# Four graph layers on one core: where roots, weight scales, kept pairs, block sums and score rows stand in the engines' order

## What is computed

```python
h = jnp.maximum(_layernorm(x, axis=-1), 0.0)
x = x + relu(dinv * (adj + I) * dinv.T @ h @ W0)                      # layer 0, dinv from row sums + 1
x = x + (dis * adj * dis.T @ h) @ W1.T + b1                           # layer 1, dis from row sums
x = x + relu(A_norm @ h @ W2)                                         # layer 2, adj + I, normalized
hw = h @ W_sa; scores = s_left[:, None] + s_right[None, :]            # layer 3, from hw
e = where(adj != 0, exp(-leaky_relu(scores, 0.01)), 0)
x_a = (e / (e.sum(1) + 1e-5)) @ hw;  x_b = adj @ (h @ W_gcnb) + b_gcnb
x = x + sigmoid(attn_a * x_a + attn_b * x_b)                          # attn_a, attn_b: sigmoid gates of adj @ h and h
```

## Time and profile before

| | |
|---|---|
| Time, median of three | 1823.18 us (1820.59 to 1827.55) |
| Profiled execution | 1826.1 us |
| Its span from first to last instruction | 1824.3 us |
| PE busy | 1710.0 us, 94% of the span |
| DVE busy | 1117.9 us, 61% |
| ACT busy | 772.5 us, 42% |
| POOL busy | 608.5 us, 33% |
| DMA | 418.91 MB, mean 230 GB/s |

### The profile page before, as it was taken

How to read it: one execution, slowest core, us unless ns; L and a number is a source line. 1 busy time by engine, 2 the same in 40 slices (tenths; PEclk the granted TensorE clock), 3 DMA queues, 4 the chain that set the end, 5 groups by cost and what they waited for, 6 DMA issues and landing times.

```text
span 1824.3 us, 31720 instructions
## 1 busy us (share of the span) xinstructions
PE 1710.0 (94%) x12862; PEld 1165.6 (64%) x12862; DVE 1117.9 (61%) x1957; ACT 772.5 (42%) x1178; POOL 608.5 (33%) x567
## 2 busy tenths in 40 slices
PE   3999898898899998999999999999999899999996
PEld 1444343655678886868877897887888544444454
DVE  5776978875676665634534443454641667877765
ACT  5665545543443433412322231310110567768654
POOL 0001636353645453522302120111210445545431
PEclk9999999999999999999999999999999999999998
DMA  9984679778958787995575798767645443444423
GB/s 393 359 308 150 217 267 316 248 277 315 329 198 294 266 308 232 326 349 209 169 251 176 227 323 312 269 216 239 224 142 170 135 127 96 147 129 119 145 85 124
DMA packets 185720, 418.91 MB, mean 230 GB/s; under 512 B 18245, under 2 KB 79041, under 8 KB 181841
## 3 DMA queue, kind: packets, MB, share of 16 engines
q1 hardware_dynamic: 185572, 416.88, 66.6%
HBM read 305.64 MB, written 111.17 MB: 228 GB/s over the span
## 4 chain that ended last, share of the span: by engine, by line
PE 67%; DVE 14%; DMA 7%; ACT 5%; POOL 3%; issue 2%; SPq 1%; ACTq 0%; DVEq 0%; POOLq 0%
PE ps L1109 13%; PE ps L1154 11%; PE ps L1156 11%; PE ps L1155 11%; PE ps L1201 7%; PE ps L1203 6%; PE ps L1202 6%; DVE U L1454 4%; DMA U<-in_adjT 3%; DMA Ad<-U 2%; ACT U L1782 1%; DMA U<-in_adj 1%; POOL U L1960 1%; DMA HB<-in_wg 1%; DVE stage L1437 1%
## 5 line engine op out<-in xcount | busy, mean ns | idle before, releaser
L1154 PE MATMUL ps<-U,HB 128*128 128x256 f16 (+2 forms) x2520 | 634.4, 260 | 7.0 <-DVE U L1454 3.6
L1155 PE MATMUL ps<-U,HB 128*128 128x256 f16 (+2 forms) x2520 | 634.2, 260 | 0.0
L1156 PE MATMUL ps<-U,HB 128*128 128x256 f16 (+2 forms) x2520 | 634.1, 260 | 0.0
L1201 PE MATMUL ps<-U,HB 128*128 128x512 f16 (+3 forms) x960 | 343.9, 361 | 47.4 <-DVE U L1454 34.7
L1202 PE MATMUL ps<-U,HB 128*128 128x512 f16 (+3 forms) x960 | 342.7, 360 | 0.0
L1203 PE MATMUL ps<-U,HB 128*128 128x512 f16 (+3 forms) x960 | 342.4, 359 | 0.0
L1454 DVE SCALAR_TENSOR_TENSOR U<-U,cS 128x512 f16<-128x512 f32 (+7 forms) x255 | 253.2, 1018 | 124.3 <-ACT U L1782 123.8
L1109 PE MATMUL ps<-W,OT 128*128 128x512 f16 (+1 forms) x1320 | 303.7, 384 | 15.5 <-DVE xr L1523 9.0
L1782 ACT ACTIVATE U<-U,cS 128x512 f16<-128x512 f32 (+7 forms) x255 | 197.5, 802 | 177.8 <-POOL U L1960 57.5
L1154 PEld LDWEIGHTS ps<-U,HB 128*128 128x128 f16 x2520 | 246.2, 98 | 36.5 <-DVE U L1454 3.8
L1155 PEld LDWEIGHTS ps<-U,HB 128*128 128x128 f16 x2520 | 246.4, 98 | 26.1
(11 more groups left out here) (204 smaller groups left out, 1954.7 us busy)
## 6 DMA issues: line engine op xcount, KB each, us to landing
U<-Ad SPq DMA_DIRECT2D x85, 896.0 KB, 6.5
U<-in_adjT SPq DMA_DIRECT2D x289, 256.0 KB, 4.6
Ad<-U SPq DMA_DIRECT2D x34, 896.0 KB, 5.8
xd<-xr SPq DMA_DIRECT2D x84, 256.0 KB, 5.7
HB<-HBd SPq DMA_DIRECT2D x24, 896.0 KB, 8.7
xr<-xd SPq DMA_DIRECT2D x84, 256.0 KB, 5.3
U<-in_adj SPq DMA_DIRECT2D x14, 1354.0 KB, 8.6
U<-Ad SPq DMA_DIRECT2D x23, 707.0 KB, 5.0
```

The lines of the kernel that those rows point to most:

```text
L1154: eng.matmul(o, h[0], hi, start=J == 0 and a == 0, stop=False)
L1155: eng.matmul(o, h[0], lo, start=False, stop=False)
L1156: last = eng.matmul(o, h[1], hi, start=False, stop=to in "acg" and J == 9 and a == 1)
L1201: eng.matmul(o, h[0], hi, start=j == 0, stop=False)
```

## The change

Nothing that is computed changes. The list of stages does:

- `AHEAD` has 18 pairs, not 20 (the pairs (6, 6) and (8, 4) are made on the fly in pass 1). They follow one another every 7.8 planned us, not 8.5; inside a pair the sums stand at 7.5, not 5.2, the splits at 11 and 12, not 8 and 9, and the write of the finished pair at 20 (15 for the last two), not 12.5.
- The square root on ACT becomes a stage of its own, "root". For the first seven pairs of layer 1's tiles it stands 2.6 planned us behind the variance, and the norms 2.6 behind that. `quiet` is 12 everywhere, where it was 16 for these. "x_keep" stands at 9, not 10.
- The power-of-two scale of a weight matrix becomes a stage "w_scale"; the high half on ACT follows two to four steps later, and all later stages of a matrix move back.
- The restores of layer 1 are cut in two DMAs: slots 0 to 3 of `HB` (free as soon as column 5 has used them) from step (5, 2J + 2) on, slots 4 to 6 from (5, 7 + J) on. Before, both went as one from (5, 11 + J) on.
- `spaced` puts two projects, not three, into the half-wide columns 10 and 16 and four, not three, into columns 11 and 17, and moves those of columns 6, 12 and 18 forward (8, 11.5, 15, 18.5 for 9, 13, 17, 21).
- The score row of column 24 is made at step (23, 8), not (23, 13); scores, masks and splits of pass 4 may stand 17, 15 and 12 planned us ahead (15.6, 13, 10.4 before), and the masks no longer wait in the list for `acc` to be free (POOL still waits for it).

```diff
--- before.py
+++ after.py
@@ -117,7 +117,7 @@
 AHEAD = [(g, j) for g in range(GW, 12) for j in
-         ((0, 2, 4, 6) if g == GW else (0, 2, 4) if g < 11 else (0, 2, 4, 10))]
+         ((0, 2) if g == 8 else (0, 2, 4) if g < 11 else (0, 2, 4, 10))]
 def made_ahead(g, j):
@@ -277,13 +277,13 @@
     def ahead(u):
         nonlocal fetched, eyed, split, summed, scored, masked
-        while scored < len(scores) and near(scores[scored], u, 6, 15.6) and scored < masked + 2:
+        while scored < len(scores) and near(scores[scored], u, 6, 17) and scored < masked + 2:
             if not have(("row_out", scores[scored][1]), *free_of("sc_a")):
                 break
             put("score", *scores[scored][1:])
             scored += 1
-        while masked < scored and near(scores[masked], u, 5, 13) and masked < s.count.get("split_e", 0) + 3:
-            if not have(("fetch",) + scores[masked], *free_of("em"), *free_of("acc")):
+        while masked < scored and near(scores[masked], u, 5, 15) and masked < s.count.get("split_e", 0) + 3:
+            if not have(("fetch",) + scores[masked], *free_of("em")):
                 break
             put("mask", *scores[masked][1:])
             masked += 1
@@ -298,7 +298,7 @@
                 break
             put("eye", *eyes[eyed][1:])
             eyed += 1
-        while split < len(splits) and near(splits[split], u, LA, 10.4 if splits[split][1] >= GE else 9.6):
+        while split < len(splits) and near(splits[split], u, LA, 12 if splits[split][1] >= GE else 9.6):
             g, j = splits[split][1:]
             if not have(("fetch", "agg", g, j)) or splits[split] in eyes and not have(("eye", g, j)) or g < 2 and not have(("scale", g)) or g >= GE and not have(("mask", g, j)):
                 break
@@ -336,30 +336,41 @@
     def weights(n, g, *js):
-        kinds = ("w_fetch", "w_max", "w_top", "w_hi", "w_lo", "w_keep") if n else ("w_fetch", "w_max", "w_hi", "w_lo")
+        kinds = ("w_fetch", "w_max", "w_top", "w_scale", "w_hi", "w_lo", "w_keep")
+        if n == 0:
+            kinds = ("w_fetch", "w_max", "w_scale", "w_hi", "w_lo")
         for kind, j in zip(kinds, js):
             plan(AT["agg", g, 0] + j if g else AT["agg", 0, 15] + j, kind, n)
     def pair(u, l, J):
         nonlocal quiet
-        plan(max(later(u, 2.6), u + 1), "norms", l, 2 * J, 2)
-        u = max(later(u, 5.2), u + 2, quiet)
+        late = 2.6 if l == 1 and J < 7 else 0
+        if late:
+            plan(max(later(u, late), u + 1), "root", l, 2 * J, 2)
+        else:
+            put("root", l, 2 * J, 2)
+        plan(max(later(u, 2.6 + late), u + 1), "norms", l, 2 * J, 2)
+        u = max(later(u, 5.2 + late), u + 2, quiet)
         steps = [(0, "normed", l, 2 * J), (0.6, "normed", l, 2 * J + 1), (1.4, "h_sums", l, J), (5, "hi", l, J),
                  (6.5, "lo", l, J)]
         if J < 8 or l == 3 and J < 10:
             steps.append((12, "image", l, J))
         if l == 1:
             steps += [(5, "xbias", 2 * J), (5, "xbias", 2 * J + 1)]
-        steps += [(10, "x_keep", "post", l - 1, 2 * J), (10, "x_keep", "post", l - 1, 2 * J + 1)]
+        steps += [(9, "x_keep", "post", l - 1, 2 * J), (9, "x_keep", "post", l - 1, 2 * J + 1)]
         for us, *stage in steps:
             v = later(u, us)
             if J == 8 and stage[0] in ("hi", "lo", "image"):
                 v = max(v, AT["agg", 6 * l, {"hi": 1, "lo": 2, "image": 5}[stage[0]]])
             plan(v, *stage)
-        quiet = later(u, 8 if J >= 7 else 16 if l == 1 else 12)
+        quiet = later(u, 8 if J >= 7 else 12)
         if J < 8:
-            late = AT["agg", 6 * l, 4 * J - 20] if J > 5 else AT["agg", 6 * l - 1, max(2 * J + 2, 11 + J if l == 1 else 0)]
-            plan(max(later(u, 24), late), "restore", l, J)
+            gone = AT["agg", 6 * l - 1, 2 * J + 2] if J < 6 else AT["agg", 6 * l, 4 * J - 20]
+            if l > 1:
+                plan(max(later(u, 24), gone), "restore", l, J, 0, 7)
+            else:
+                plan(max(later(u, 24), gone), "restore", l, J, 0, 4)
+                plan(max(later(u, 24), gone, AT["agg", 5, 7 + J]), "restore", l, J, 4, 7)
         if l == 3 and J in (7, 9):
             plan(max(later(u, 14), AT["agg", GE - 1, 17 if J == 7 else 20]), "restore_h21", 1 if J == 7 else 2)
@@ -400,18 +411,21 @@
         g, c = now - 1, now % 6
-        at_us = {0: (9, 13, 17, 21), 4: (9, 14, 19), 5: (3, 10, 15)}.get(c, (12, 18.5, 25, 31.5))
+        at_us = {0: (8, 11.5, 15, 18.5), 4: (9, 18), 5: (3, 10, 16.5, 23)}.get(c, (12, 18.5, 25, 31.5))
+        n = 2
+        if now >= GE - 2:
+            n, at_us = 3, (9, 14, 19) if c == 4 else (3, 9, 20)
         todo = [(g, t) for t in tiles(g)]
         if c == 4:
-            todo.pop()
+            todo = todo[:n]
         if c == 5:
-            todo.insert(0, (g - 1, tiles(g - 1)[-1]))
+            todo = [(g - 1, t) for t in tiles(g - 1)[n:]] + todo
         for (f, t), us in zip(todo, at_us):
             p, v = CHUNKS[f][0], later(u, us)
             plan(v, "project", f, t, SUMS[now]["x"])
             if p < 3:
                 if c or t not in tiles(g)[:2]:
-                    plan(max(u + 1, later(u, us - 9)), "x_load", "post", p, t)
+                    plan(max(u + 1, later(u, us - (9 if c else 6))), "x_load", "post", p, t)
             post(max(v + 1, later(v, 1.5)), p, t)
         if CHUNKS[g][0] == 3:
             v = later(v, 5)
@@ -439,7 +453,7 @@
             project(u, g - 1)
         if winograd(g) and j == 19:
             put("gather", g)
-        if g < GW and g and j == 16:
+        if g < GW and g and j == (19 if g == 4 else 16):
             for t in tiles(g - 1):
                 plan(u + 1, "x_load", "post", 0, t)
         if j < NT - 1:
@@ -474,14 +488,14 @@
         put("load_adj", t)
         put("load_x", t)
     put("setup2")
-    weights(0, 0, 0, 3, 6, 7)
+    weights(0, 0, 0, 3, 6, 6, 7)
     plan(u0 + 1, "constants")
     for d, kind in enumerate(("gate_max", "gate_top", "gate_w")):
         plan(AT["agg", 2, 3] + d, kind)
-    weights(4, 2, 4, 7, 12, 13, 14, 20)
-    weights(3, 2, 21, 24, 31, 32, 33, 39)
-    weights(1, 3, 12, 15, 19, 20, 21, 27)
-    weights(2, 4, 0, 6, 14, 15, 16, 22)
+    weights(4, 2, 4, 7, 12, 13, 16, 18, 24)
+    weights(3, 2, 21, 24, 31, 32, 35, 37, 43)
+    weights(1, 3, 14, 17, 20, 21, 24, 26, 32)
+    weights(2, 4, 6, 9, 15, 16, 19, 21, 27)
     for n in range(8):
         plan(AT["agg", 2, 13] + n, "v_dot", n // 4, n % 4)
     plan(AT["agg", 3, 4], "v_keep")
@@ -490,9 +504,9 @@
     plan(AT["agg", 6, 16], "factors", 3)
     for n, (g, j) in enumerate(AHEAD):
-        u = later(AT["agg", 2, 1], 8.5 * n)
-        for us, *stage in ((0, "fetch", "pre", g, j), (0, "fetch", "pre", g, j + 1), (5.2, "sums", g, j), (8, "split", g, j),
-                           (9, "split", g, j + 1), (12.5, "a_keep", g, j)):
+        u = later(AT["agg", 2, 1], 7.8 * n)
+        for us, *stage in ((0, "fetch", "pre", g, j), (0, "fetch", "pre", g, j + 1), (7.5, "sums", g, j),
+                           (11, "split", g, j), (12, "split", g, j + 1), (20 if n < 16 else 15, "a_keep", g, j)):
             plan(later(u, us), *stage)
     for _, g, j in SEQ:
         if GW <= g < 12 and j == whole(j) and fly(g, j):
@@ -513,7 +527,7 @@
         plan(u + 2, "xhalf", t)
         plan(u + 3, "x_keep", "dot", 3, t)
     for g in range(GE, G):
-        first = AT["agg", g - 1, 13 if g == GE else 10 if g == GE + 1 else 6]
+        first = AT["agg", g - 1, 8 if g == GE else 10 if g == GE + 1 else 6]
         for i in range(CHUNKS[g][2]):
             plan(first + (i if g > GE else 0), "row", g, i)
         plan(first + (CHUNKS[g][2] + 1 if g > GE else 1), "row_out", g)
@@ -886,7 +900,7 @@
             if l == 4 and slot == S1:
                 return s_h21[J // 4], 16
             l = min(l, 3)
-            return (s_hb[J], 16 * l) if J < 8 else (s_plo, s("lo", l, J))
+            return (s_hb[J], 16 * l + 16) if J < 8 else (s_plo, s("lo", l, J))
         def plain_slots(j):
@@ -1018,17 +1032,17 @@
                     eng.dma_start(HBd[l][a:b, :, J, :, :].rearrange("s p h n -> p s (h n)"),
                                   stage[:, n % 2, a:b, :, :].rearrange("p s h n -> p s (h n)")).then_inc(s_kept[n % 2], 16)
                 elif kind == "restore":
-                    l, J = of
+                    l, J, a, b = of
                     for at_kept in images_kept(image_no(l, J) + 1):
                         sync.wait_ge(*at_kept)
                     sync.wait_ge(s_agg, s("agg", 6 * l - 1, 2 * J + 1))
-                    if l == 1:
+                    if l == 1 and b == 7:
                         sync.wait_ge(s_wlo, 5)
                         sync.wait_ge(s_wkept, 64)
                         sync.wait_ge(s_vdot, 8)
-                        sync.wait_ge(*KEPT[[a for a in AHEAD if LANE[("pre",) + a] == 7][-1]])
-                    eng.dma_start(HB[:, :, J, :, :].rearrange("p s h n -> p s (h n)"),
```

(17 more changed lines are left out.)

## The result

The changed kernel takes 1830.4 us (median of 8 runs, 1827.2 to 1831.5), the kernel before beside it 1822.6. The ratio is 1.0038 with a 95% interval of 1.0026 to 1.0050: **a little slower**, by some 7 us, where 1786 was forecast and 1765 to 1815 held for likely.

What follows compares the result with a forecast made beforehand. PE bounds the kernel, busy 94% of the span; columns 2 to 4 are bound by waits between ACT and DVE. Terms sum to 37.1 us: 1826.1 profiled becomes 1789.0, or 1786 against the median 1823.2; range 1765 to 1815.

Steps and rivals of the forecast that it cites:

- Columns 2 and 3: Roots, scales, kept pairs, block sums: PE idle falls from 22.1 to 8 us, plus 2.3 of clock; gain 16.4.
- The wait for weight 1's fetch: Matrices' stages, column 3: a new wait for weight 3's low half; loss 1.5 us, bounds 0 and 4.
- DVE's need: Columns 2 and 3: DVE's work falls from 132.6 to 127.0 us, against PE's 137.3 less 2.3 of clock.
- The write of kept pairs: Layer 0: with the write planned 8 us behind the split, SP, which stood 68.8 us, goes on to queued fetches.
- Columns 4 and 5: Column 4 loses root and scale waits: gain 3.4 us; column 5, two pairs fewer, restores in two parts: gain 5.0.
- Column 6: Projects earlier; pair (6, 6)'s 2.8 us on DVE hidden by DVE's idling; gain 5.0 us, bounds -6 and 11.7.
- layer 1 starts late: Rival: SP standing at column 5's restores delays column 6's fetches, price 18 us; total 1839; chance 0.06.
- Column 8: Pair (8, 4) costs 2.8 us of DVE beside a busy PE; -0.5 us, 0 to -3.
- Column 10: Second project's wait for the first's post goes, splits are late next; gain 4.0 us, bounds 0 and 9.1.
- Columns 11 and 12: Third project moves to column 11, same 2.6 us of PE; column 12's split passes block sums; gain 2.0 us.
- everything closes: Rival: PE's gaps go and the late starts behind them too; 63 us gained, total 1760; chance 0.13.
- Column 24: Score rows and masks earlier: start maybe some 2 us later, 3.69 us gap goes; gain 3.3, bounds -3 and 7.7.

Runs made afterwards that it cites:

- y1: Changed kernel with weight 3's scale and halves earlier, weight 1's fetch two steps earlier and its spread one step later; 1824.3 us, ratio 1.0000.
- x4_row: Changed kernel with score rows, scores, masks, last splits and column 23's projects put back as before; 1827.6 us, ratio 1.0012.
- w1: Changed kernel with the write of a kept pair planned 4.5 us after its split instead of 9; 1827.3 us, ratio 1.0015.
- y2: Changed kernel with the roots put back, taken at once instead of 2.6 us later, norms 2.6 us earlier; 1842.0 us, ratio 1.0091.
- y3: Changed kernel with all stages of the four weights back at the steps of the kernel before; 1825.1 us, ratio 0.9997.
- x2: Changed kernel with pair (8, 4) made ahead again, 19 pairs; 1823.5 us, ratio 0.9988.
- w3: Changed kernel with pair (6, 6) made ahead again, 19 pairs; 1828.8 us, ratio 1.0026.
- x3: Changed kernel with the projects of half-wide columns, from column 6 on, where they stood before; 1825.6 us, ratio 1.0004.
- w2: Changed kernel with the image write of layer 1's pair 7 planned 20 us behind its norms instead of 12; 1826.8 us, ratio 1.0013.
- u2: Changed kernel with the four projects of columns 11 and 17 at 2, 7, 12, 17 us instead of 3, 10, 16.5, 23; 1829.7 us, ratio 1.0027.
- z6: z1 with pair 7's image behind the fetches of column 6 and column 10's pair writes three steps earlier; 1810.3 us, ratio 0.9920.
- x1_weight1: Changed kernel with weight 1's largest entry planned later on DVE; 1829.9 us, ratio 1.0023.
- z1: Changed kernel with the edits of y1, x2, x3 and x4_row combined; 1812.8 us, ratio 0.9933.

## Why the prediction was wrong

By its own terms, in us gained between the landmarks. The sum was 37.1. By columns the traces give -3.6; the changed kernel came to column 2 1.8 us sooner, for which there was no term, and the whole is -1.3.

**Columns 2 and 3: 16.4 less 1.5 forecast, 1.7 measured.** The largest miss. Three steps of it failed.
- *The wait for weight 1's fetch.* The mechanism was foreseen (a fetch one step before the low half that it waits for), its price was not: -1.5 with a bound of -4, where PE stood 6.13 us with 6.8 us of half clock behind it (5.25 us of busy PE in them, so 2.6 lost). y1 shows 5.7 us at column 4. The bound of 4 us went by the waiting of DVE alone. The chain is fetch, landing (7.0 us from issue), largest entry (2.29), spread on PE, and PE waits for its end; I counted steps between stages on one engine and not between the first and the last.
- *DVE's need.* 127.0 us were computed, 134.9 measured (69.20 + 65.73), where before had 133.8 between the same marks. Of this the splits are one part. In columns 2 and 3 the second tile of a pair (768 wide) went from 1.16 to 1.63 us in the buffer `U`, and from 1.21 to 1.40 in `HB`. Before, and then the two tiles after:
```profile
L1454 DVE SCALAR_TENSOR_TENSOR U<-U,cS 128x768 f16<-128x768 f32 x6 | 7.0, 1164 | 0.0
...
L1468 DVE SCALAR_TENSOR_TENSOR U<-U,cS 128x1024 f16<-128x1024 f32 x6 | 9.8, 1634 | 0.3 <-ACT U L1797 0.3
L1468 DVE SCALAR_TENSOR_TENSOR U<-U,cS 128x768 f16<-128x768 f32 x6 | 9.8, 1626 | 0.0
```
 The prices of the earlier trace rows were taken as fixed, but the earlier trace rows had shown that they depend on what POOL does meanwhile. The timelines bear it out: with POOL idle such a split of 768 takes 1.01 us in both kernels (six of 12 before, one of 11 after), with POOL busy all through it 1.61 before (two) and 1.84 after (six). The Trainium skill ("GPSIMD Engine Reference", Specifications) has VectorE contend with GpSimd at two SBUF inputs; the trace agrees, by these numbers. Why the splits meet POOL more often is open: no run moved the block sums alone. The 12.2 us over the program are another matter. 7.9 of them fall behind the start of column 23, among masks and their splits, and x4_row takes 6.9 back (1123.2 us).
- *The write of kept pairs.* "SP goes on to the fetches": it doesn't, 68.8 us became 71.2 one instruction further. The danger that was named, the buffer released later, came: 29.0 us of ACT's waits. w1 is 4 us faster without it.

These three leave a part of the 13 us open: y1, without the first of them, still gains 7.4 us by column 4 where 14.9 were forecast, with its next gap (4.73 us) at a split. What was right there is the reading of the earlier trace rows: the exchange between ACT and DVE. y2 puts 10 us on the roots alone. Without this the change would have been 17 us slower than before.

**Columns 4 and 5: 3.4 and 5.0 forecast, 3.1 and 3.6 measured.** Column 4 is right, by the causes given: with the roots put back (y2) it is 0.8 us longer than before, with the scales put back (y3) 0.1 shorter. Column 5 is near in size. With one of the two pairs put back (x2, w3) it takes 57.1 and 55.8 us, where before took 55.2, the kernel after 51.6 and x3, in the same order as the latter, 54.5. So most of the gain seems to hang on the pairs. What the restores in two parts are worth no run shows.

**Column 6: 5.0 forecast, -0.6 measured.** The cover named ("DVE idles at this place until the transfers have landed") was there, 6.98 us of it, but it lay before the pair (6, 6) and not beside it: the pair's own fetch was what DVE idled for. w3 and w2 each bring the 6 us. The gap at the last pair of tiles did shrink, from 4.55 to 3.53 us. The rival "layer 1 starts late" had the right queue, SP, and the wrong instruction on it: an image, not a restore.

**Column 8: -0.5 forecast, -7.5 measured.** The second largest miss. The 2.8 us of DVE were laid beside a busy PE and nothing else counted. The step that failed is that a pair on the fly also needs a raw slot, the buffer of its fetched tiles: with one pair more the fetches wait longer for DVE to free one. From 554 to 592 us SP stands 25.2 us in such waits, against 18.8 in x2 between 555 and 592. POOL idles 6.77 us for the landing, DVE 5.64 behind it, and PE 4.54 for the post:
```profile
579.77 1.26 POOL L1975 TENSOR_TENSOR U<-U 128x512 f32<-128x512 f32 x1 [6.77 <-DMA U<-in_adjT]
```
```profile
582.25 1.47 DVE L1468 SCALAR_TENSOR_TENSOR U<-U,cS 128x1024 f16<-128x1024 f32 x1 [5.64 <-ACT U L1797]
```
That the pair is the cause x2 settles, with 7.9 us; that the slot is the link is read from the traces.

**Column 10: 4.0 forecast, 2.4 measured** (5.0 less the 2.6 of the project that moved to column 11). Near in its cause, and the split next in line was named (4.21 us).

**Columns 11 and 12: 2.0 forecast, -6.0 measured** (12.5 less 3.9 less 2.6). The third project was said to cost "the same 2.6 us of PE there". It also puts a post, a norm and its writes into a column where DMA is 0.95 busy, and ACT's gather behind that norm. x3 and u2 take the gap ahead of column 12 away, and pay elsewhere: the limit is the transfers of kept pairs, which the text held against "everything closes" and not against its own term.

**Column 24: 3.3 forecast, -0.3 measured.** Both effects were named and the one was sized wrong: the start came not "some 2 us" but 6.9 us later (gates behind 5.6 us of DVE for masks and their splits), with half the clock from 1432.1 on; the inner gap and its half clock, 6.6 us, went as said.

Of the signs listed, ACT's waits for wR gone and those for the variance under 12 us came, and no half clock near 220, and one stretch of gaps, not two, at column 24. SP's waits at the write (L1012 before, L1026 after) went as the sign says, but only to the next fetch, so the sign was a poor one. PE idle for 8 us in columns 2 and 3 did not come (it was 6.1 + 12.9 = 19.0); and two of the three signs of "wrong" were there, a wait of ACT for the kept pair's write and one of DVE for the weight's fetch. The case as it came is none of the four rivals. The error was common to the terms: each priced the engine on which a stage runs and not the buffer or the transfer that it shares. What stays open is where the longer executions of the changed kernel have the half clock that its profiled one has not.

## What to carry to other kernels

A wait that is split or moved is worth what its whole chain leaves: count from the first issue (here a fetch) to the last waiter on the bound engine, through every buffer, before a stage in the middle is put later. Where three engines each run in fixed order, work that looks hidden beside the bound engine should be priced by the slots it takes, because a fetch that waits for a slot holds all that is queued behind it. Try the parts one by one: here one move of 2.6 us was worth 10 us and one pair cost 8, and the sum hid both.

## What the runs showed that was not expected

- SP's standing for the splits of pairs made ahead is conserved: 68.8 us in 15 waits before, 71.2 in 13 after, 68.9 in 14 with the writes early. Whichever instruction stood next waited; that it is DVE's pace which sets this is argued from these three, not shown.
- The same 1957 instructions of DVE take 1117.9 us in one order (before, and z6), 1130.1 in that of the kernel after, and 1123.2 in that with only the score rows undone.
- The length of a gap alone didn't tell whether half the clock came behind it, so "each such gap of 3 us or more brings half clock" in the prediction does not hold. The one of 2.77 us in the earlier trace rows was followed by 3.4 us of it, and one of 3.69 us at the same place of y1_weight_gap (PE's post at step 5 of column 6) by none. In the kernel after 3.20 us were followed by 6.8 us of half clock, in x1_weight1 1.42 us by none, and with the same steps and the same work column 6 took 72.7 and 66.7 us. The gap of 3.53 us (3.52 in z1) at step 20 of column 6 stands in both of these and in others: it was followed by no half clock in x1 and z1, by 3.4 us of it in the kernel after, w2 and w3, and by 6.8 us in x3 and x4.
